# Local attention on one core: the order of the score matmuls within a slot

## Chip, core and metric

One NeuronCore of a Trainium2 chip runs the whole program. The metric is the device time of one execution in microseconds; the kernel before takes 2629.06 us (median of three runs, 2627.81 to 2631.6).

## What is computed

The input is x with 8 sequences of 256 tokens and 128 channels, 2048 tokens in all. Four blocks follow one another, each with a layer norm before and after it and a residual: additive attention, a six-layer transformer with local attention, a state-space scan, and a mixture of 8 experts. The change is in the second one. Of each of its six layers, this is the part that matters (b sequences, 16 heads of 64 dims, windows of 32 queries which see the 64 keys of their own window and the one before):

```
q, k, v = split((shift_tokens(x)) @ Wqkv)          # 128 -> 3 x 1024
q, k = rotary(l2norm(q) * qs), rotary(l2norm(k) * ksc)
sim  = einsum('bhwie,bhwje->bhwij', bq, bk2) * 8.0  # bq: (.., 32, 64), bk2: (.., 64, 64)
sim  = where(mask, -finfo.max, sim)
out  = einsum('bhwij,bhwje->bhwie', softmax(sim), bv2)
x    = out @ Wo + x
x    = ffn(shift_tokens(x)) + x                     # 128 -> 2 x 341 -> 128, gated by GELU
```

## The kernel before

Everything is in float32 unless said otherwise, with channels on partitions and tokens along the free dimension. The local-attention block works on units of 512 tokens (two sequences): 6 layers of 4 units, 24 units. A unit is worked through in 8 slots j = 0 to 7, and slot j is about the pair of heads 2j and 2j+1, of which one lies on partitions 0 to 63 and the other on partitions 64 to 127. So there are 192 slots, one score phase in each.

Each engine has its own program, written out by hand as a function `slot(i, j, ...)` (TensorE L529, ScalarE L643, GpSimd L715, VectorE L793) that is called from `iterations` (L347). The units 1 to 22 lie in a hardware loop whose body holds two units. The engines meet through semaphores alone, and each works through its list strictly as written (`need` and `gather` are waits). Work is pipelined over the slots: in slot j TensorE does the scores of pair j, the q and k projections and their norms for pair j+2, the value projection, the product with the values for pair j-2, and the transposes of pair j-1. The output projection (`wo_part`, L491) and the feed-forward part of the previous unit are spread over the slots.

TensorE in a slot, in order: `scores` (L439: two mask matmuls at L450, then the 32 score matmuls at L457); the projections `project` (L430, L431) into banks 0 and 1; `values` (L418); `mix` (L478); parts of the output projection or feed-forward (L491 to L525); `turn` (L466, transposes); `norms` (L436, L437). In slot 2 a part of L491 comes before the projections; in slot 6 L511 and `mix` do.

The score phase itself. Before it stand two waits, for the q and k of this pair (written by VectorE, L757) and for the probabilities of the pair before (written by VectorE, L781), because the score banks are used again. The two mask matmuls write the bfloat16 mask into bank 4 (head 0) and bank 5 (head 1). Each head then has 16 windows. The matmul of window w of head h takes 64 dims (partitions 64h to 64h+63) by 32 queries as weights, 64 keys as moving data, and adds into partitions 32(w mod 4) to 32(w mod 4)+31 of bank 4+h. The array is thus used in tiles of 64 rows by 32 columns: h chooses the row half, w mod 4 one of four column groups. In the trace each of these float32 matmuls is two weight loads and two matmul records, 64 of each in a slot. `mix` (L478) has two heads too, alternating; its tiles are 64 rows by 64 columns, head h in row half h and column half h, so there are two of them, and its loop is written with the head inside.

After the score phase of pair j: VectorE takes the row maximum (L765) and subtracts it (L769), ScalarE takes the exponential (L663), VectorE sums, inverts and multiplies (L776, L779, L781). ScalarE's copy of the projections (L607) and its square (L610) stand ahead of the exponential in ScalarE's list. VectorE also has the normalising product (L757) and the shuffle for the rotary embedding (L747, L750) in every slot, and in some slots residual, shift and layer-norm work. Two of these matter here: at the end of its slot 2 the residual (L816) and the shifted input of the feed-forward part (L726, L728), and at the end of its slot 5 the shifted input xs of the next unit (L726, L728), which that unit's first projection waits for (L430, in slot 6). VectorE gets to both when TensorE is already in the slot after. GpSimd does the other half of the rotary products (L709, L713).

Of the kernel before, what the change touches and what calls it, by code (L numbers as in the profile page):

```python
# [29 lines left out]
DEPTH, HEADS, DH, WIN = 6, 16, 64, 32  # L30
INNER = HEADS * DH
NP = HEADS // 2
UNIT = 512
# [11 lines left out]
def view(buf, col, *pattern, p0=0, rows=128):  # L45

    a = buf[p0:p0 + rows, 0:1]
    return bass.AP(a.tensor, a.offset + col, [[a.ap[0][0], rows]] + [list(x) for x in pattern])
# [246 lines left out]
def local_attention(nc, io, x, con):  # L295
# [9 lines left out]
    with Pool(nc) as m:  # L305
# [93 lines left out]
        def _(pe):  # L399
            def gather(sm_, value):  # L400

                if not isinstance(value, int) or value > 0:
                    pe.wait_ge(sm_, value)
                    pe.sem_inc(sem["seen"], 1)
# [34 lines left out]
            def scores(i, j):  # L439

                gather(sem["qk"], i * 8 + j + 1)
                gather(sem["p"], i * 8 + j)
                if isinstance(i, int) and i + j == 0:
                    pe.wait_ge(n1.out, n1.n + NCH)
                    pe.sem_inc(sem["seen"], 1)
                    pe.wait_ge(sem["zero"], 2)
                    pe.sem_inc(sem["seen"], 1)
                t = qk[j % 2]
                for h in range(2):
                    pe.matmul(view(ps, (4 + h) * CH, [1, 256]), identb[:, :], maskb[:, :], start=True, stop=False,  # L450
                              skip_group_check=True)
                for h in range(2):
                    for w in range(UNIT // WIN):

                        keys = (view(t, KOFF + WIN * w, [-WIN, 2], [1, WIN], p0=64 * h, rows=64) if w % 2 == 0
                                else view(t, KOFF + WIN * (w - 1), [1, 2 * WIN], p0=64 * h, rows=64))
                        mm = pe.matmul(view(ps, (4 + h) * CH + (w // 4) * 64, [1, 64], p0=WIN * (w % 4), rows=WIN),  # L457
                                       t[64 * h:64 * h + 64, WIN * w:WIN * w + WIN], keys, start=False, stop=True,
                                       skip_group_check=True)
                mm.then_inc(sem["s_mm"], 1)  # L460
# [68 lines left out]
            def slot(i, j, run, more, before):  # L529
# [4 lines left out]
                if run:  # L534
                    scores(i, j)
# [1119 lines left out]
```

## Time and profile before

| | us |
|---|---|
| median of three runs | 2629.06 (2627.81 to 2631.6) |
| span of the profiled execution | 2628.3 |
| median of the runs less this span (what lies around it) | 0.8 |
| TensorE matmul busy | 2396.4 (91%) |
| TensorE weight load busy | 1259.7 (48%) |
| VectorE busy | 1953.7 (74%) |
| ScalarE busy | 1795.4 (68%) |
| GpSimd busy | 1082.1 (41%) |

The local attention with its feed-forward runs from about 100 to 2076 us. A busy time is the union of the records of an engine. TensorE's records overlap: the next matmul of the same shape starts well before the record of the last one ends, so starts say more about its rate than lengths do.

### The profile page before, as it was taken

The numbers are of one execution on the slowest core, as the hardware profiler recorded it, in microseconds if no ns is written. First come the engines' busy times: TensorE is split into PE (matmuls) and PEld (weight loads), VectorE is DVE, ScalarE is ACT, GpSimd is POOL, SyncE is SP. The second block draws the span as 40 slices with busy tenths as digits, with TensorE's granted clock in tenths as the row PEclk, the third lists the DMA queues.
The fourth block names the chain that finished last, engine by engine and source line by source line (L and its number), as shares of the span: only waits on it lengthen the run. The fifth ranks groups of instructions, "written<-read, shape, count | busy, mean of one in ns | idle before, by whom it ended". The sixth has DMA issues, their size and how long they took to land. (4 is left out here: it accounts for less than half of the span.)

```text
span 2628.3 us, 62460 instructions
## 1 busy us (share of the span) xinstructions
PE 2396.4 (91%) x24940; PEld 1259.7 (48%) x24940; DVE 1953.7 (74%) x2595; ACT 1795.4 (68%) x2593; POOL 1082.1 (41%) x461
## 2 busy tenths in 40 slices
PE   7799999999999999999999999999999877767778
PEld 2355555555554555555545455555555422222355
DVE  5678777788677777787778777788777658999542
ACT  4677767777677776777767777677677666545533
POOL 0354444444444444444444444444444204556130
PEclk8899999999999999999999999999999989999989
DMA  0100000000000000000000000000000010000001
GB/s 21 54 2 2 2 26 10 10 2 2 15 22 11 2 2 14 22 11 2 2 14 14 19 2 2 14 14 15 5 2 2 2 37 0 0 0 0 18 23 41
DMA packets 16047, 29.92 MB, mean 11 GB/s; under 512 B 3616, under 2 KB 6064, under 8 KB 15664
## 3 DMA queue, kind: packets, MB, share of 16 engines
q1 hardware_dynamic: 15760, 25.78, 3.1%
q8 instruction: 218, 3.57, 0.5%
q14 instruction: 69, 0.57, 0.1%
HBM read 24.73 MB, written 1.05 MB: 10 GB/s over the span
## 5 line engine op out<-in xcount | busy, mean ns | idle before, releaser
L709 POOL TENSOR_TENSOR f_rot<-f_raw,f_tabc 128x1024 f32<-128x1024 f32 x192 | 452.6, 2357 | 694.7 <-DVE f_qk L757 302.4
L713 POOL TENSOR_TENSOR f_rot<-f_rot,f_shuf 128x1024 f32<-128x1024 f32 x192 | 453.1, 2360 | 470.0 <-DVE f_shuf L750 470.0
L607 ACT ACTIVATE f_raw<-f_ps 128x1024 f32<-128x1024 f32 x192 | 196.5, 1023 | 324.9 <-PE f_ps L431 324.9
L478 PEld LDWEIGHTS f_ps<-f_ptz,f_v 64*64 64x64 f32 x6144 | 260.2, 133 | 93.7 <-issue 93.7
L478 PE MATMUL f_ps<-f_ptz,f_v 64*64 64x96 f32 (+1 forms) x6144 | 286.7, 243 | 1.5 <-ACT f_ptz L628 1.4
L776 DVE TENSOR_REDUCE f_sum<-f_ps 128x8 f32<-128x512 f32 x192 | 131.8, 686 | 185.6 <-ACT f_ps L663 185.5
L747 DVE STREAM_SHUFFLE f_shuf<-f_raw 128x1024 f32<-128x1024 f32 x192 | 255.2, 1329 | 0.0
L757 DVE SCALAR_TENSOR_TENSOR f_qk<-f_rn,f_rot 128x1024 f32<-128x1024 f32 x192 | 233.5, 1216 | 28.8 <-POOL f_rot L713 28.8
L430 PE MATMUL f_ps<-f_xs,f_wq 128*128 128x512 f32 x384 | 220.7, 657 | 24.3 <-DVE f_xs L728 21.0
L750 DVE TENSOR_TENSOR f_shuf<-f_shuf,f_tabs 128x1024 f32<-128x1024 f32 x192 | 236.7, 1233 | 7.6
L616 ACT ACTIVATE f_rn<-f_ps 128x1024 f32<-128x1024 f32 x192 | 198.8, 1035 | 39.5 <-PE f_ps L437 39.0
L618 ACT ACTIVATE f_rn<-f_rn,k_lift 128x1024 f32<-128x1024 f32 x192 | 220.6, 1149 | 6.3
L457 PE MATMUL f_ps<-f_qk 64*32 64x64 f32 x12288 | 195.1, 220 | 18.0 <-issue 18.0
L1136 POOL TENSOR_TENSOR s_prod<-s_state,s_cs 128x1024 f32<-128x1024 f32 x64 | 151.7, 2371 | 145.2 <-DVE s_state L1214 145.2
L418 PE MATMUL f_ps<-f_wv,f_xs 128*64 128x256 f32 x1536 | 210.5, 395 | 0.0
L765 DVE TENSOR_REDUCE f_max<-f_ps 128x8 f32<-128x512 f32 x192 | 131.8, 686 | 105.1 <-PE f_ps L457 103.7
L610 ACT ACTIVATE f_sq<-f_raw 128x1024 f32<-128x1024 f32 x192 | 203.1, 1058 | 6.1
L436 PE MATMUL f_ps<-f_sq,f_same 128*128 128x512 f32 x384 | 197.7, 597 | 6.2 <-ACT f_sq L610 6.2
L431 PE MATMUL f_ps<-f_xs,f_wk 128*128 128x512 f32 x384 | 203.1, 611 | 0.0
L437 PE MATMUL f_ps<-f_sq,f_same 128*128 128x512 f32 x384 | 197.0, 595 | 0.0
L457 PEld LDWEIGHTS f_ps<-f_qk 64*32 64x32 f32 x12288 | 161.9, 106 | 60.2 <-issue 60.2
L491 PE MATMUL f_ps<-f_o,f_wo 128*128 128x512 f32 x384 | 183.8, 612 | 0.0
(267 smaller groups left out, 3961.4 us busy)
## 6 DMA issues: line engine op xcount, KB each, us to landing
e_w<-in_e_w SPq DMA_DIRECT2D x16, 256.0 KB, 2.8
f_wq<-in_f_wq SPq DMA_DIRECT2D x12, 256.0 KB, 2.8
f_wk<-in_f_wk SPq DMA_DIRECT2D x12, 256.0 KB, 3.2
f_wv<-in_f_wv SPq DMA_DIRECT2D x12, 256.0 KB, 3.4
f_wo<-in_f_wo SPq DMA_DIRECT2D x6, 512.0 KB, 3.1
f_w<-in_f_w SPq DMA_DIRECT2D x6, 341.0 KB, 3.1
s_dx<-in_k_pick SPq DMA_DIRECT2D x1, 1536.0 KB, 9.3
f_w<-in_f_w SPq DMA_DIRECT2D x6, 192.0 KB, 3.8
```

The lines of the kernel that those rows point to most:

```text
L418: mm = pe.matmul(view(ps, 2 * CH + 256 * r, [1, 256], p0=64 * h, rows=64), xs[:, at:at + 64], view(wv, CH * (q // 4) + 64 * h, [128, 4], [ ...
L430: pe.matmul(bank(0), wq[:, 128 * j:128 * j + 128], xs[:, :], start=True, stop=True)
L431: pe.matmul(bank(1), wk[:, 128 * j:128 * j + 128], xs[:, :], start=True, stop=True).then_inc(sem["a_mm"], 1)
L457: mm = pe.matmul(view(ps, (4 + h) * CH + (w // 4) * 64, [1, 64], p0=WIN * (w % 4), rows=WIN), t[64 * h:64 * h + 64, WIN * w:WIN * w + WIN] ...
L478: mm = pe.matmul(view(ps, 7 * CH + 64 * p, [1, n], p0=64 * h, rows=64), v[64 * h:64 * h + 64, p * CH + 64 * j:p * CH + 64 * j + 64], ptz[6 ...
L610: act.activation(sq[:, :], raw[:, :], ACT.Square).then_inc(sem["sq"], 1)
L618: act.activation(rn[:, :], rn[:, :], ACT.Exp, scale=-0.5, bias=con.lift).then_inc(sem["rn"], 1)
L709: pool.tensor_tensor(view(rot, 0, [S, 4], [1, S]), view(raw, 0, [S, 4], [1, S]), view(tab_c, 0, [S, 2], [0, 2], [1, S]), ALU.mult).then_in ...
L713: pool.tensor_tensor(rot[:, :], rot[:, :], shuf[:, :], ALU.add).then_inc(sem["rot"], 1)
L747: dve.stream_shuffle(shuf[:, :], raw[:, :], [(p + 16) % 32 for p in range(32)]).then_inc(sem["shuf"], 1)
L750: dve.tensor_tensor(view(shuf, 0, [S, 4], [1, S]), view(shuf, 0, [S, 4], [1, S]), view(tab_s, 0, [S, 2], [0, 2], [1, S]), ALU.mult).then_i ...
L757: dve.scalar_tensor_tensor(out=view(qk[j % 2], 0, [KOFF, 2], [1, UNIT]), in0=view(rn, 0, [UNIT, 2], [1, UNIT]), scalar=1e12, in1=view(rot, ...
```

## The change

Within a slot, the loop over the two heads is moved inside the loop over the 16 windows. The 32 score matmuls, their operands, their tiles and their outputs are the same; what differs is the order in which they are issued: (window 0, head 0), (window 0, head 1), (window 1, head 0), and so on, in place of 16 windows of head 0 and then 16 of head 1. The last one issued, which tells VectorE that the scores are there, is window 15 of head 1 in both.

```diff
                 for h in range(2):
                     pe.matmul(view(ps, (4 + h) * CH, [1, 256]), identb[:, :], maskb[:, :], start=True, stop=False,
                               skip_group_check=True)
-                for h in range(2):
-                    for w in range(UNIT // WIN):
+                for w in range(UNIT // WIN):
+                    for h in range(2):
 
                         keys = (view(t, KOFF + WIN * w, [-WIN, 2], [1, WIN], p0=64 * h, rows=64) if w % 2 == 0
                                 else view(t, KOFF + WIN * (w - 1), [1, 2 * WIN], p0=64 * h, rows=64))
```

## Rows read from the trace of the kernel before

**Rows 1.** Busy time by engine in the local attention (windows): length, then each engine
```profile
100.00:2076.00 1976.00, 1897.38 (x23356) 1035.79 (x23340) 1529.52 (x2128) 1465.70 (x2133) 896.91 (x381) 0.99 0.03 9
```

**Rows 2.** Groups by line, TensorE: busy us, mean ns | idle before, releaser
```profile
L478 PE MATMUL f_ps<-f_ptz,f_v 64*64 64x96 f32 (+1 forms) x6144 | 286.7, 243 | 1.5 <-ACT f_ptz L628 1.4
L457 PE MATMUL f_ps<-f_qk 64*32 64x64 f32 x12288 | 195.1, 220 | 18.0 <-issue 18.0
```

**Rows 3.** Timeline of TensorE over one slot: start, length, line, count
```profile
1045.39 0.99 PE L457 MATMUL f_ps<-f_qk 64*32 64x64 f32 x64
1046.31 1.12 PE L430 MATMUL f_ps<-f_xs,f_wq 128*128 128x512 f32 x2
...
1049.24 1.49 PE L478 MATMUL f_ps<-f_ptz,f_v 64*64 64x96 f32 x32
1050.66 0.66 PE L466 MATMUL f_ps<-f_ident,f_s 128*128 128x128 f32 x4
```

**Rows 4.** L457's matmuls in that slot, stretches from its start: length, busy (records)
```profile
1045.38:1045.66 0.28, 0.27 (x20) 1.00 0.00 0
1045.38:1045.83 0.45, 0.44 (x40) 1.00 0.00 0
1045.38:1046.17 0.79, 0.78 (x64) 1.00 0.00 0
```

**Rows 5.** L457, first 0.03 us of that phase: count, duration ns min/median/max
```profile
L457 PE MATMUL f_ps<-f_qk x4: 240/240/240, 1045.4 to 1045.4; 64*32 64x64 f32 x4
```

**Rows 6.** Records in flight in 0.01 us: of L478, then of L457 twice
```profile
1009.20:1009.21 0.01, 0.01 (x6) 1.00 0.00 0
1045.84:1045.85 0.01, 0.01 (x25) 1.00 0.00 0
1046.12:1046.13 0.01, 0.01 (x16) 1.00 0.00 0
```

**Rows 7.** Slots 1, 2, 3, 4 and 6 of one unit, as Rows 1
```profile
1349.88:1360.40 10.52, 10.46 (x125) 5.75 (x124) 6.55 (x9) 6.83 (x10) 4.96 (x3) 1.00 0.24 76
1360.40:1369.91 9.51, 9.51 (x123) 5.37 (x122) 4.34 (x8) 6.67 (x10) 4.47 (x2) 1.00 0.01 2
1369.91:1379.77 9.86, 8.91 (x122) 4.93 (x121) 9.64 (x14) 7.11 (x12) 3.90 (x2) 1.00 0.01 2
1379.77:1388.41 8.64, 8.64 (x120) 4.99 (x121) 7.71 (x12) 7.19 (x12) 5.48 (x3) 1.00 0.01 2
...
1398.00:1409.89 11.89, 10.84 (x125) 5.52 (x124) 11.43 (x19) 10.61 (x16) 5.16 (x3) 1.00 0.01 1
```

**Rows 8.** Waits over the whole span: us in total, times, longest us
```profile
DVE f_max L765 <- PE f_ps L457: 103.7, 58, 2.8
PE f_ps L450 <- DVE f_s L781: 33.6, 51, 2.4
PE f_ps L430 <- DVE f_xs L728: 21.0, 24, 5.3
PE f_ps L457 <- issue: 18.0, 10, 2.1
```

**Rows 9.** Timeline of VectorE in slots 2, 3 and 4 of that unit
```profile
1368.97 0.69 DVE L781 TENSOR_TENSOR f_s<-f_ps,f_rcp 128x512 f32<-128x512 f32 x1
...
1375.51 0.69 DVE L765 TENSOR_REDUCE f_max<-f_ps 128x8 f32<-128x512 f32 x1
...
1378.93 0.69 DVE L781 TENSOR_TENSOR f_s<-f_ps,f_rcp 128x512 f32<-128x512 f32 x1
...
1386.18 0.69 DVE L776 TENSOR_REDUCE f_sum<-f_ps 128x8 f32<-128x512 f32 x1 [0.24 <-ACT f_ps L663]
...
1387.14 0.69 DVE L781 TENSOR_TENSOR f_s<-f_ps,f_rcp 128x512 f32<-128x512 f32 x1
```

**Rows 10.** ScalarE, slot 4: the copy of the projections that the exponential stands behind
```profile
1383.02 1.02 ACT L607 ACTIVATE f_raw<-f_ps 128x1024 f32<-128x1024 f32 x1 [1.39 <-PE f_ps L431]
```

**Rows 11.** TensorE at the head of slot 0 of that unit, timeline
```profile
1338.84 0.64 PE L457 MATMUL f_ps<-f_qk 64*32 64x64 f32 x11 [1.55 <-issue]
```

## Prediction, made before the changed kernel ran

> **What bounds the kernel now.** I read the busy times first. In the local attention TensorE has a matmul under way 1897 of 1976 us, 96%, VectorE 77%, ScalarE 74%, GpSimd 45% [rows 1]. That is an average; what a shorter score phase is worth depends on whether TensorE or another engine ends last in each of the eight slots. For this the windows of one unit: in slots 1, 2 and 4 TensorE's busy time fills the slot, in slots 3 and 6 it lacks 0.95 and 1.05 us, and there VectorE is at 9.64 of 9.86 and 11.43 of 11.89 us [rows 7]. The waits name the places: the mask matmul waits 51 times for the probabilities (L781), about two per unit (slots 4 and 7), the first projection waits 24 times, once per unit (slot 6), for the shifted input (L728) [rows 8]. From the other side, VectorE's maximum waits for the score matmuls in only 58 of 192 slots [rows 8]: in the others VectorE comes late anyway. So TensorE bounds most of a unit, and VectorE two stretches of it.
>
> **What the score phase costs now.** From its first record to the start of the next group is 46.31 - 45.39 = 0.92 us [rows 3], of which 0.79 us lie before the start of the last of its 64 records [rows 4]. The starts come at three rates: 20 in the first 0.28 us (14 ns each), 20 more in the next 0.17 us (8.5 ns each), 24 in the last 0.34 us (14 ns each) [rows 4]. What does 14 ns mean? L478 has two tiles, and its 32 records, of 96 columns, take 50.66 - 49.24 = 1.42 us [rows 3], so a tile takes a record every 89 ns; by columns, a score record of 64 would want 59 ns. One head has four tiles, which gives 59/4 = 15 ns, about the 14 seen. So the first and the last stretch are one head at the speed of its four tiles, and the middle one is both heads at once. The records in flight say the same: 25 in the middle, 16 at the end [rows 6]. Head 0's 32 records at 14 ns fill 0.45 us; head 1 needs as long, but begins 0.28 us late, since it stands behind 32 others in the order.
>
> **The change part by part.** Nothing is added: 32 score matmuls in 64 records with as many weight loads, in each of 192 slots, no wait, no semaphore, no DMA. What moves is the order, and with it the idle half of the array at both ends of the phase. No other queue is passed, and the last matmul is the same, so the signal to VectorE means what it meant.
>
> The gain per slot, from both sides. If all eight tiles are fed from the first record, the phase lasts as long as one head alone, 32 x 14 ns = 0.45 us, plus a few tens of ns: the last start moves from 0.79 to about 0.48, 0.31 us saved. If instructions can't be supplied faster than in the stretch in which both heads ran, it is 64 x 8.5 ns = 0.54 us, 0.25 us saved. Since that is a rate that this order has been seen to run at, and 0.45 is one that it has not, I take 0.54, so **0.25 us per slot**. At the other end stands the loss: the nearest other phase with alternating heads, L478, has just 6 records in flight [rows 6], two tiles' worth. If alternation meant two tiles at a time here as well, 32 pairs x 59 ns = 1.89 us, 1.10 us more than now. I don't take it, because L478 has no more than two tiles to fill, while the scores have four per head, and 25 in flight in the middle stretch show more than four tiles at work. The ends are thus +1.10 and -0.31, and the value is near the second because its row is of this very phase.
>
> How many slots pass it on? I follow one unit, by what each stretch waits for.
> - Slots 7, 0, 1, 2: behind slot 7's mask TensorE has no further wait of the kinds in [rows 8] up to slot 4's mask, but for the ten breaks below; each score phase lies between two pieces of its own work. Four savings pass.
> - Slot 3: its scores don't matter. VectorE finishes the probabilities of slot 2 (L781 at 1368.97 + 0.69), then goes through shuffle, products, residual and shift and takes the maximum of slot 3 only at 1375.51 [rows 9], 4.3 us after the scores; its probabilities come at 1378.93 + 0.69, and the mask of slot 4 starts at 1379.77 [rows 7, 9]. VectorE's stretch between them has no score phase in it. It starts earlier by what was saved before, so nothing is lost either.
> - Slot 4: TensorE is full again, one saving. The other path, to slot 4's probabilities, must also come earlier: the exponential stands behind ScalarE's copy, which waits 1.39 us for the projection and so moves by the whole saving [rows 10], and VectorE's sum waits 0.24 us for the exponential [rows 9]. So that path gives 0.24, and it has room: the probabilities are there at 1387.14 + 0.69 [rows 9], 0.58 us before the mask of slot 5 at 1388.41, where slot 4 ends [rows 7].
> - Slots 5 and 6: TensorE is full in slot 5, but then waits in slot 6 for the shifted input, and that wait grows by slot 5's saving. Slot 6's scores lie before that wait too. So neither of the two passes. What was saved in slots 7 to 4 does pass through this stretch, since VectorE's list from the probabilities of slot 4 to that shift starts earlier by it.
>
> Five of eight, in 24 units: 120 savings. In ten slots the score phase breaks off after 53 records and waits for its own instructions, 18.0 us in all [rows 8], as in slot 0 of that unit, where the last 11 come 1.55 us late [rows 11]; the supply comes when it comes, and a faster start only waits longer. 110 x 0.25 = **27 us**. Against the span of 2628.3 us that is 2601; the median of the runs is 0.8 us above the span, so **2602 us**. With 0.31 us in all 120 it would be 37 us less, 2592.
>
> What could be late next is what TensorE meets sooner after a shorter phase: the projections need banks 0 and 1 free of ScalarE's reads, and the products need the spread probabilities. For the second, all of L478's idle time is 1.5 us in 192 slots [rows 2]; I take both as covered.
>
> A rule stands against all this. The first four records of the phase start within 0.03 us and all last 240 ns, where the mean is 220 [rows 2, 5]. The Trainium skill says in "TensorE: Matmul & The Clock Gate", section Part 3 (packing small matmuls), that matmuls start and end strictly in program order and that only weight loads are pulled ahead. By that rule a window's second record would wait for its first in the same tile, all behind it too, and the phase would need 32 x 59 ns = 1.9 us in either order; the change would be worth nothing. The 0.79 us measured [rows 4] speak against it: tiles evidently don't hold each other up.
>
> **The rivals.**
> - *A, no change in the phase.* If the middle stretch is fast only because a backlog of head 0 is worked off, while new instructions arrive every 14 ns, then any order takes 64 x 14 ns = 0.9 us less a backlog at the start, which is what it takes now. For it: the last 24 starts at 14 ns. Against it: they are explained by head 1's four tiles, 16 in flight [rows 6]. Time 2629.
> - *B, the phase is shorter, but less passes on.* The margins near the chain are close to the saving: 0.24 us at slot 4's sum [rows 9]. If the savings of slots 4 and 7 are lost to VectorE, three per unit less the ten stalls, 62 x 0.25 = 15.5 us, are left: 2613.
> - *C, slower: two tiles at a time.* If TensorE looks ahead less far than the eight tiles' instructions, so that a second window of the same head is not reached while the first runs, each slot loses 1.10 us. It decides from the point at which fewer than four tiles are busy. Price: 110 or more times 1.10 = 121 us, 2750. For it: L478's alternating order with 6 in flight [rows 6]. Against it: head 1's records start now while head 0 still has 12 of its 32 to go, that is over a distance of at least 12 matmuls and their weight loads.
> - *D, all eight tiles from the start.* The 37 us above, 2592. For it: four tiles do start within 0.03 us [rows 5].
>
> **How the numbers follow.** The forecast has 0.56, D 0.12, B 0.14, A 0.11, C 0.07. Measurement tells about 0.2% (5 us) from no change. Faster takes the forecast, B and D: 0.82; same 0.11; slower 0.07. The range leaves out A and C and takes in the bounds of the first three: 2589 to 2619.
>
> **What would show it.** In the changed trace L457's 64 records should start within 0.50 to 0.56 us, with 25 to 32 in flight nearly throughout; 0.79 again means A, over 1.5 us C. The busy time of L457 should fall from 195 us [rows 2] by 192 x 0.25 = 48 to about 147. The maximum's wait for the scores falls in slots 0 to 2. TensorE's waits for L781 should not fall, since slots 4 and 7 stay VectorE's, and its wait for L728, 21.0 us now, should grow by about 24 x 0.5 us, the unused savings of slots 5 and 6. If the phase is 0.25 us shorter and the time falls by less than 20 us, B holds and the sum over slots is wrong. If the time falls by more than 40 us, slots that I put on VectorE's account were TensorE's after all.

## The result and the profile after

The changed kernel takes 2613.1 us (median of 4 runs, 2611.19 to 2614.84), the kernel before in the same comparison 2629.98 us (4 runs): ratio 0.9938, 95% interval 0.9926 to 0.9949, so 13 to 19 us less. Forecast were 2602 us, with 2589 to 2619 as the range. Five more runs of the same kernel gave 2610.47 us, ratio 0.9924 (0.9911 to 0.9937) against 17 runs of before. The gain is there; it is some 17 to 19 us and not 27. One run of a later kernel (unroll_alt_1356, below) took 3398 us at a granted clock of 0.649; it is left out of every comparison, and all others agree within 0.4% with the median of their kernel.

From the page of the changed kernel, its busy times and the groups of `mix` and of the scores (busy us, mean ns | idle before):

```profile
PE 2374.6 (91%) x24940; PEld 1232.9 (47%) x24940; DVE 1954.8 (75%) x2595; ACT 1797.4 (69%) x2593; POOL 1083.0 (41%) x461
...
L478 PE MATMUL f_ps<-f_ptz,f_v 64*64 64x96 f32 (+1 forms) x6144 | 286.4, 243 | 1.5 <-ACT f_ptz L628 1.4
...
L457 PE MATMUL f_ps<-f_qk 64*32 64x64 f32 x12288 | 167.8, 225 | 19.5 <-issue 19.5
```

L457 is busy 195.1 - 167.8 = 27.3 us less than in [rows 2], 0.14 us per slot, where 48 us were forecast. The timeline of the slot that answers to [rows 3]:

```profile
1040.02 0.86 PE L457 MATMUL f_ps<-f_qk 64*32 64x64 f32 x64
1040.80 1.13 PE L430 MATMUL f_ps<-f_xs,f_wq 128*128 128x512 f32 x2
```

The next group starts 0.78 us after the first record, 0.92 before. How the 64 starts spread, as in [rows 4] (stretch from the phase's start, length, busy, records):

```profile
1040.01:1040.26 0.25, 0.24 (x32) 1.00 0.00 0
1040.01:1040.29 0.28, 0.28 (x33) 1.00 0.00 0
1040.01:1040.40 0.39, 0.39 (x38) 1.00 0.00 0
1040.01:1040.57 0.56, 0.55 (x57) 1.00 0.00 0
1040.01:1040.66 0.65, 0.65 (x64) 1.00 0.00 0
```

Half of the records start in 0.24 us, which is all eight tiles at full speed. Then there is a pause: one record up to 0.28 us, five more up to 0.39 us, and the remaining 26 in the last 0.26 us, 10 ns each. The median over the 192 phases, from first to last start, is 0.642 us after and 0.778 before: **0.136 us saved per slot**, forecast 0.25.

The slots of the unit that answers to [rows 7] (slots 1, 2, 3, 4 and 6, windows from mask to mask):

```profile
1341.60:1352.12 10.52, 10.32 (x126) 5.61 (x125) 6.60 (x9) 6.83 (x10) 4.32 (x3) 1.00 0.23 76
1352.12:1361.49 9.37, 9.37 (x123) 5.23 (x122) 4.35 (x8) 6.68 (x10) 4.53 (x2) 1.00 0.01 2
1361.49:1371.32 9.83, 8.77 (x121) 4.78 (x120) 9.61 (x14) 7.11 (x12) 3.89 (x2) 1.00 0.01 3
1371.32:1379.84 8.52, 8.52 (x121) 4.86 (x122) 7.72 (x12) 7.21 (x12) 5.37 (x3) 1.00 0.01 2
1389.42:1401.31 11.89, 10.70 (x126) 5.39 (x125) 11.43 (x19) 10.62 (x16) 5.16 (x3) 1.00 0.00 1
```

Slots 2 and 4 are 0.14 and 0.12 us shorter than in [rows 7], slots 3 and 6 are what they were, as forecast. Slot 1 is 10.52 us in both, and that was not forecast. Its TensorE busy time fell by 0.14 us and its length by nothing. The timeline of slot 1 names the reason (TensorE and ScalarE lines):

```profile
1341.60 0.38 PE L450 MATMUL f_ps<-f_maskb,f_identb 128*128 128x256 bf16 x2
...
1341.80 1.02 ACT L616 ACTIVATE f_rn<-f_ps 128x1024 f32<-128x1024 f32 x1 [0.63 <-PE f_ps L437]
...
1341.91 0.86 PE L457 MATMUL f_ps<-f_qk 64*32 64x64 f32 x64
...
1342.97 1.10 PE L430 MATMUL f_ps<-f_xs,f_wq 128*128 128x512 f32 x2 [0.20 <-ACT f_rn L616]
```

ScalarE's Ln (L616) reads banks 0 and 1, which the norms of the slot before have just filled and which the projection L430 is to write. It begins when the norms end, takes 1.02 us, and only then may L430 start. The score phase lies beside it, and a shorter one only uncovers the wait. It was the same before: in slot 1 of the unit of [rows 7] L430 also followed the Ln, 1.06 us after the first score record, where in [rows 3] it was 0.92.

```profile
1350.08 1.02 ACT L616 ACTIVATE f_rn<-f_ps 128x1024 f32<-128x1024 f32 x1 [0.63 <-PE f_ps L437]
1350.19 0.99 PE L457 MATMUL f_ps<-f_qk 64*32 64x64 f32 x64
...
1351.25 1.10 PE L430 MATMUL f_ps<-f_xs,f_wq 128*128 128x512 f32 x2
```

In the changed kernel it is 1342.97 - 1341.91 = 1.06 us again, with a score phase that is 0.14 us shorter. Over the units this stretch has the same median, 1.06 us, in slots 1 and 3 of both kernels, and goes from 0.92 to 0.79 us in slots 4 and 5. The wait now stands among the waits of the changed kernel, 47 times, in slots 1 and 3 of the units:

```profile
PE f_ps L450 <- DVE f_s L781: 34.0, 51, 2.4
...
PE f_ps L430 <- DVE f_xs L728: 24.2, 24, 5.3
PE f_ps L457 <- issue: 19.5, 10, 2.6
...
PE f_ps L430 <- ACT f_rn L616: 9.4, 47, 0.2
```

All masks of the two traces, grouped by slot, give the whole account (sum over 24 units, 23 for slot 7, since no mask follows the last one; median of units 1 to 22; worked out from the starts of L450):

| slot | before, median us | after, median us | sum saved, us |
|---|---|---|---|
| 0 | 10.48 | 10.33 | 5.6 |
| 1 | 10.52 | 10.52 | 0.0 |
| 2 | 9.51 | 9.37 | 3.1 |
| 3 | 9.84 | 9.85 | -0.3 |
| 4 | 8.65 | 8.51 | 3.2 |
| 5 | 9.58 | 9.59 | 0.0 |
| 6 | 11.89 | 11.88 | -0.1 |
| 7 | 11.24 | 11.10 | 4.4 |

Slots 2 and 4 give 24 x 0.136 = 3.3 us less a bit. Slot 7 has some 1.2 us more than its 23 x 0.136 = 3.1 us. In slot 0 the 14 units without a break give 1.8 us, about 14 x 0.136 = 1.9, and the ten others 3.8 us. So about 12 us are placed (3 x 24 + 14 = 86 savings), and the rest sits in slots 7 and 0, where the hardware loop branches back.

### The profile page after: what moved, and what is told of

The parts are those of the page before. It is cut to its first block and busy times, and to the rows that moved or that the text cites. A ratio compares the mean times of both kernels' runs of the same rounds, so it can differ in the third digit from the quotient of the medians.

```text
span 2613.1 us, 62460 instructions
## 1 busy us (share of the span) xinstructions
PE 2374.6 (91%) x24940; PEld 1232.9 (47%) x24940; DVE 1954.8 (75%) x2595; ACT 1797.4 (69%) x2593; POOL 1083.0 (41%) x461
## 5 line engine op out<-in xcount | busy, mean ns | idle before, releaser
L478 PEld LDWEIGHTS f_ps<-f_ptz,f_v 64*64 64x64 f32 x6144 | 260.1, 133 | 93.9 <-issue 93.9
L478 PE MATMUL f_ps<-f_ptz,f_v 64*64 64x96 f32 (+1 forms) x6144 | 286.4, 243 | 1.5 <-ACT f_ptz L628 1.4
L430 PE MATMUL f_ps<-f_xs,f_wq 128*128 128x512 f32 x384 | 216.1, 645 | 34.3 <-DVE f_xs L728 24.2
L616 ACT ACTIVATE f_rn<-f_ps 128x1024 f32<-128x1024 f32 x192 | 199.0, 1036 | 38.9 <-PE f_ps L437 38.6
L765 DVE TENSOR_REDUCE f_max<-f_ps 128x8 f32<-128x512 f32 x192 | 132.0, 687 | 97.7 <-PE f_ps L457 96.2
L437 PE MATMUL f_ps<-f_sq,f_same 128*128 128x512 f32 x384 | 197.0, 595 | 0.0
L457 PE MATMUL f_ps<-f_qk 64*32 64x64 f32 x12288 | 167.8, 225 | 19.5 <-issue 19.5
L418 PEld LDWEIGHTS f_ps<-f_wv,f_xs 128*64 128x64 f32 x1536 | 94.6, 138 | 164.5 <-issue 135.4
```

Source lines behind the costliest of these rows:

```text
L418: mm = pe.matmul(view(ps, 2 * CH + 256 * r, [1, 256], p0=64 * h, rows=64), xs[:, at:at + 64], view(wv, CH * (q // 4) + 64 * h, [128, 4], [ ...
L430: pe.matmul(bank(0), wq[:, 128 * j:128 * j + 128], xs[:, :], start=True, stop=True)
L478: mm = pe.matmul(view(ps, 7 * CH + 64 * p, [1, n], p0=64 * h, rows=64), v[64 * h:64 * h + 64, p * CH + 64 * j:p * CH + 64 * j + 64], ptz[6 ...
L616: act.activation(view(rn, 0, [UNIT, 2], [1, UNIT]), bank(0, 2), ACT.Ln, scale=float(2.0 ** 20)).then_inc(sem["ln"], 1)
```

## The experiments

Three questions: what sets the 0.64 us of the phase; which slots pass a saving on; and what the rest beyond 12 us is. The diffs show little more than the lines that change.

**The change once more**, unedited:

> The changed kernel once more, to set the noise. Theory S (supply): the score phase is limited by how fast its instructions come; a second trace must then show the same 0.64 us from the first to the last start of its 64 records in all slots that don't break off, since nothing else enters. The savings of 0.136 us should again lie in slots 2, 4 and 7 and in those slots 0 without a break, and none in slots 1, 3, 5 and 6; the broken slots 0 should differ from the first trace by up to 3 us either way. Rival N (the missing gain is noise): slot 1 or the phase length varies between traces. Time 2613, ratio 0.9926 to 0.9949.

2610.47 us (five runs, 2606.31 to 2610.57), ratio 0.9924 (0.9911 to 0.9937). The phase is 0.642 us again, slots 1, 2, 4 and 7 have the same medians to 0.002 us, and the sum of slot 0 differs by 3.7 us from the first trace (276.4 against 280.1). Theory N falls: neither the phase nor slot 1 varies. What varies from run to run is slot 0, and slot 6 of the very first unit (11.78 against 13.38 us).

**Half the windows**, to see the phase without its second 64 instructions. Windows 8 to 15 of both heads aren't computed in these two kernels (of the second only the new line is shown, in the place of the same two):

```diff
-                for h in range(2):
-                    for w in range(UNIT // WIN):
+                for w, h in [(w, h) for w in range(8) for h in range(2)]:
+                    if True:
```

> Windows 8 to 15 of both heads are left out (16 score matmuls, 32 records); the other windows alternate between the heads. Theory S: the first 64 instructions (32 loads, 32 records) stand ready when the phase begins and go at the tiles' speed, so the last start is 0.24 us after the first. Rival U (one rate for the whole phase, that of the changed kernel): half of 0.64 us, 0.32 us. The time of the whole is not compared; this is for the length of the phase.

```diff
+                for w, h in [(w, h) for h in range(2) for w in range(8)]:
```

> The same 16 score matmuls (windows 8 to 15 left out), first all of head 0, then all of head 1. In the kernel before, head 1 begins 0.27 us late, at its 65th instruction; here its first instruction is the 33rd. Theory S1: what is in the queue can start whatever stands before it; head 1 then starts within 0.05 us of head 0, and the order makes no difference, 0.24 us. Theory S2: TensorE reaches about 32 instructions past the oldest one that has not started; head 1 then comes in with the second round of head 0, at about 0.08 to 0.13 us, and the last start is at 0.32 to 0.36 us.

First to last start: 0.238 us alternating, 0.265 us head by head. The starts of each, alternating first (stretch from the phase's start, records):

```profile
1006.99:1007.23 0.24, 0.23 (x30) 1.00 0.00 0
1006.99:1007.24 0.25, 0.24 (x32) 1.00 0.00 0
```
```profile
1009.13:1009.40 0.27, 0.26 (x31) 1.00 0.00 0
1009.13:1009.41 0.28, 0.27 (x32) 1.00 0.00 0
```

One rate for the whole phase (0.32 us) is out. The second kernel bears on my main question. In the kernel before, head 1 comes in 0.27 us late; here, with head 0 only half as long, it comes in after 0.05 us, its 16 records then running beside head 0's. So a second head as such isn't held back. Two readings are left of why it came late in the kernel before: it stood at instruction 65 (32 loads and 32 records before it), or head 0 had too many records waiting for its four tiles. The kernel by_group, below, decides for the second. In these two half kernels, of 64 instructions each, the order is worth 0.03 us. The Trainium skill gives TensorE in "TensorE: Matmul & The Clock Gate" (the table at the head of the page) a queue of 64 instructions. The changed kernel is in line with it: its first 64 instructions, 32 records, go at the tiles' speed, the last of them starting at 0.238 us, and the next two records start at 0.27 and 0.32 us (medians of the 192 phases). That these 64 are the queue isn't shown.

**Where in the phase the order counts.** All 32 matmuls, alternating in the first or in the second half only:

```diff
+                for w, h in [(w, h) for w in range(8) for h in range(2)] + [(w, h) for h in range(2) for w in range(8, 16)]:
```

> All 32 score matmuls: windows 0 to 7 alternating, then windows 8 to 15 of head 0, then of head 1. Theory S: the first half goes as in the changed kernel (32 records by 0.24 us), then matmuls come at 17 ns each; head 0's eight take 8 x 28 ns on its four tiles, head 1's come meanwhile: last start 0.64 to 0.72 us. Theory T (tiles alone decide, supply doesn't): second half 2 x 0.22 less the overlap, 0.24 + 0.30 to 0.45 = 0.54 to 0.69 us.

```diff
+                for w, h in [(w, h) for h in range(2) for w in range(8)] + [(w, h) for w in range(8, 16) for h in range(2)]:
```

> All 32 score matmuls: windows 0 to 7 of head 0, then of head 1, then windows 8 to 15 alternating. Theory S: what comes after the first 64 instructions is bound by their arrival, 17 ns a matmul, as in the changed kernel, so the order of the first half hardly matters: last start 0.64 us, time as the changed kernel's, 2613. Theory T: the first half takes 0.32 us or more instead of 0.24, and all after it is pushed back by the same: 0.70 us or more.

Both phases last 0.686 us; one run each gave 2626.3 and 2618.5 us (2613 expected for the second), with 2630.9 us for the kernel before beside them. The two stretches of each, first_alt first:

```profile
1045.90:1046.18 0.28, 0.27 (x33) 1.00 0.00 0
1045.90:1046.60 0.70, 0.69 (x64) 1.00 0.00 0
```
```profile
1042.93:1043.21 0.28, 0.27 (x33) 1.00 0.00 0
1042.93:1043.63 0.70, 0.69 (x64) 1.00 0.00 0
```

In both, as in the changed kernel, 33 records have started by 0.28 us, although the first 64 instructions stand in different orders. After it all three go slower, and differently. For first_alt the range of theory S holds, and so, just, does that of T (0.54 to 0.69). For second_alt S said 0.64 and T at least 0.70; 0.686 is neither. That the arrival of instructions is what holds the second half fits the first half being alike, but it isn't shown, and 0.045 us of second_alt I can't explain. Of the 0.136 us, either half alone gives 0.092.

**Fewer tiles at a time**, the mechanism of my slower rival made real:

```diff
+                for w, h in [(4 * k + g, h) for g in range(4) for k in range(4) for h in range(2)]:
```

> The kernel before, but the windows ordered by column group: 0, 4, 8, 12, then 1, 5, 9, 13 and so on, heads alternating. The same 32 matmuls; eight successive ones share two tiles. Theory S with a reach of about 32 instructions (eight matmuls with their loads): two tiles work at a time, 32 pairs x 56 ns = 1.8 us from first to last start, 1.0 us more than before; in slots 0, 2, 4, 7 all of it and in the others a part passes: 2730 to 2780. With a reach of 64 instructions four tiles work, 16 rounds x 56 ns = 0.9 us: about 2645. If tiles don't matter and only the supply does, 0.64 us as in the changed kernel: 2613.

```profile
1061.99:1062.27 0.28, 0.28 (x12) 1.00 0.00 0
1061.99:1063.20 1.21, 1.21 (x64) 1.00 0.00 0
```

12 records in the first 0.28 us in place of 20, and 1.20 us in all, between the two theories' 1.8 and 0.9; the time of its one run is 2663.4 us, also between the 2730 to 2780 and the 2645 of the two. So the order can also cost, 0.42 us per slot and 33 us in all: the same matmuls, with successive ones sharing tiles. My two guesses of how far TensorE reaches past a waiting instruction (32 and 64 instructions) both miss.

The starts in this trace also tell why head 1 came late in the kernel before. A record that finds its tile unused lasts 240 ns, as the first four in [rows 5] do; one in a tile that is in use lasts 216 ns. So the records of 240 ns show when new tiles come in (medians over the 192 phases, worked out from starts and lengths; the counts are the same in at least 191 of them):

| kernel | tiles at work | records given to them | started when new tiles come in | not yet started, per tile | time, us |
|---|---|---|---|---|---|
| before | 4 | 32 | 20 | 3 | 0.27 |
| half_heads | 4 | 16 | 4 | 3 | 0.05 |
| by_group, 2nd pair of tiles | 2 | 16 | 10 | 3 | 0.26 |
| by_group, 3rd pair | 2 | 16 | 10 | 3 | 0.52 |
| by_group, 4th pair | 2 | 16 | 10 | 3 | 0.78 |

The second pair of tiles in by_group begins with instruction 33, as head 1 does in half_heads, and comes in 0.21 us later. So the place in the order doesn't decide, and the 64 instructions aren't needed to explain it. What all five have in common is the backlog: new tiles come in when the tiles ahead of them have three records each left to start. With alternating heads the first 32 records are four per tile, one running and three left, and no new tile is kept out. The pause after them in the changed kernel is another matter. Its 33rd record is the fifth of its tile, and starts at 0.27 us; in the kernel before and in by_group the fifth record of a tile starts at 0.25 us, on time. So that pause isn't the tile's, and what is left is the place behind the first 64 instructions.

**Which slots pass it on.** The value projection, which uses bank 2, goes before the q and k projections in slots 1 and 3, as it does in slot 7 already:

```diff
-                    if j == 7:
+                    if j in (1, 3, 7):
                         values(u, a)
                     project(u, a)
-                    if j != 7:
+                    if j not in (1, 3, 7):
                         values(u, a)
```

> The changed order of the scores, and in slots 1 and 3 TensorE does the value projection (L418) before the q and k projections, as it already does in slot 7. Theory P: in slots 1 and 3 the saving of the score phase is lost because the first projection waits for ScalarE's Ln (L616), which still reads banks 0 and 1; with the value projection in between, that wait is covered. Slot 1 should then be shorter by about 0.24 us (in slot 7 of the changed kernel mix starts at 4.024 us from the mask, in slot 1 at 4.268), slot 3 by nothing, since VectorE ends last there. 24 x 0.24 = 6 us: 2607. Rival Q: slot 1 is bound by ScalarE's work (copy, square, exponential), which the later projections push back by 1 us; then 2613 or more.

> The order of the scores before the change, with the value projection first in slots 1 and 3. Theory P: slot 1 gains only what TensorE waited there before the change, 4.268 - 4.160 = 0.11 us, so 24 x 0.11 = 2.6 us: 2627; and the difference to the same kernel with alternating heads is now 24 x 0.136 = 3 us larger than 17 us, because slot 1 passes its saving too: 20 us. Rival Q: no change against before, 2630, or slower, and the difference stays 17 us.

Slot 1's median: 10.28 us with alternating heads (10.52 without this edit), 10.41 us head by head (10.52). That is 0.24 and 0.11 us, to the digit what theory P said, and slot 3 is unchanged. TensorE in slot 1 of v13_alt has no wait left:

```profile
1344.98 0.86 PE L457 MATMUL f_ps<-f_qk 64*32 64x64 f32 x64
1345.77 1.08 PE L418 MATMUL f_ps<-f_wv,f_xs 128*64 128x256 f32 x8
1346.78 1.13 PE L430 MATMUL f_ps<-f_xs,f_wq 128*128 128x512 f32 x2
```

The times hardly show it: 2610.31 us (2607 expected), ratio 0.9924 (0.9907 to 0.9940), and 2629.3 us (2627 expected), 0.9999 (0.9990 to 1.0007). The first kernel's runs spread from 2600.83 to 2616.73 us, and slot 0 has 284.2 us in its trace, 4 to 8 more than in the two traces of the changed kernel. Between the two kernels lie 19.0 us by the medians, 20 expected; by the two traces it is 12.3 us from the first mask to the last, with nothing gained in slot 0 (283.4 and 284.2 us). The breaks had to go before anything of this size could be timed.

**Without the loop.** The units 1 to 22 written out in place of a hardware loop:

```diff
-            with eng.Fori(0, (LAST - 1) // 2) as pair:
-                for i in (pair * 2 + 1, pair * 2 + 2):
-                    for j in range(8):
-                        slot(i, j, True, True, True)
+            for i in range(1, LAST):
+                for j in range(8):
+                    slot(i, j, True, True, True)
```

The second kernel adds the change; the third alternates in slots 1, 3, 5 and 6 alone (`sorted(order) if j in (1, 3, 5, 6) else order`); the fourth is the second with the value projection first in slots 1 and 3.

> The order of the scores before the change; the hardware loop over units 1 to 22 is written out, so that no engine branches back. Theory B: the ten breaks in slot 0 come with the branch back at every second unit; each costs (1.12 - 0.43) us before the mask and (3.45 - 1.24) us up to the first projection, 2.9 us, 29 us in all: 2601. Rival F: the instructions come as slowly in a straight line, and breaks appear elsewhere: 2630 or slower.

> The same written-out units, with the alternating order. Theory P (the saving is 0.136 us a slot and passes in slots 0, 2, 4 and 7 alone): with no breaks it is 24 x 4 x 0.136 = 13 us against unroll_heads: 2588. If the 3 to 7 us that the change gave beyond the 12 us that I can place belong to the breaks, the difference is 13 us here; if they belong to something else in the attention, it is 16 to 20 us.

> Written-out units; the heads alternate in slots 1, 3, 5 and 6 only, the other four slots have the order before. Theory P: all four phases are 0.136 us shorter and none passes it on (slot 1 waits for the Ln at banks 0 and 1, slots 3, 5 and 6 for VectorE): the time of unroll_heads, 2601, within 1 us. Rival (my prediction's sum): slot 1 passes its saving, 3.3 us less. If all eight pass theirs, 13 us less.

> Written-out units, alternating order, and the value projection first in slots 1 and 3. Theory P: slot 1 is 0.24 us shorter again, 24 x 0.24 = 5.8 us less than unroll_alt: 2582, the fastest so far. Rival: as in the looped pair, where slot 1 was 0.24 us shorter but the whole no faster, the time stays that of unroll_alt.

| kernel | median us | ratio to before | interval |
|---|---|---|---|
| unroll_heads | 2582.69 | 0.9821 | 0.9809 to 0.9834 |
| unroll_alt_1356 | 2580.02 | 0.9812 | 0.9799 to 0.9824 |
| unroll_alt | 2570.40 | 0.9771 | 0.9758 to 0.9783 |
| unroll_v13_alt | 2565.18 | 0.9756 | 0.9743 to 0.9769 |

The ten breaks are gone and no others appear; 48 us are saved, not 29, since I had priced a break only up to the first projection, while the sum of slot 0 alone falls from 285.6 to 248.2 us, slot 7 by 6.9 and slot 6 by 5.0 us. Slot 7 is shorter only in the ten units ahead of a branch back, but slot 6 in all units 1 to 22, by 0.3 us (11.89 to 11.59); so about 5 of the 48 us aren't at the branch, and why slot 6 gains isn't shown. Here the change is worth 2582.69 - 2570.40 = **12.3 us**, against 13 worked out. By slot 0 to 7 it saves 3.5, 0.0, 3.1, -0.1, 3.2, -0.1, -0.4 and 3.1 us. Alternating in slots 1, 3, 5 and 6 alone shortens those phases too (L457 busy 178.4 us, against 191.8 and 165.1), and the sums of slots 0 to 5 and 7 stay within 0.4 us; the time is 2.7 us less, by itself nearer to the rival's 3.3. But slot 1's sum is 249.8 us in both; slot 6 has 1.5 us, all of it in the first unit, and about 1.1 us lie before the attention. The value projection first takes 5.2 us more off (5.8 expected), 4.8 of them in slot 1. Slots 1 and 2 of unroll_alt, as in the rows above:

```profile
1311.72:1322.24 10.52, 10.32 (x126) 5.61 (x125) 6.57 (x9) 6.82 (x10) 4.68 (x3) 1.00 0.23 76
1322.24:1331.61 9.37, 9.37 (x123) 5.23 (x122) 4.34 (x8) 6.67 (x10) 4.50 (x2) 1.00 0.01 3
```

The last kernel is the fastest of all, 65 us below the kernel before.

## Why the prediction came out as it did

The direction and the mechanism, more tiles at work per score phase, held, and the time lies in the range; the size was 17 to 19 us where 27 were forecast. By its steps:

- *What the three rates of [rows 4] mean.* Right as far as it went: one head is bound by its four tiles, and alternation fills the other four. The rule of strict program order among matmuls, which would have made the change worthless, is contradicted by the result too: the order made a difference.
- *The gain per slot, 0.25 us.* This is the term that was mis-sized: 0.136. I took 8.5 ns, the rate of the stretch with both heads, as one the whole phase could keep. The last records of the phase come near it, at 10 ns, but between the first 32 records and those there is a stretch from 0.24 to 0.39 us with only 6 starts, which no row of before shows. The forecast had 25 to 32 records in flight nearly throughout; there are 29 in the first stretch, but 18 and 22 in two later ones. What was missing were two things. One is why head 1 starts at 0.28 us in [rows 4]: I read it as a matter of order alone, and by_group shows that it is one of backlog, three records per tile. That part alternation removes. The other is that behind the first 64 instructions the phase goes slower in any order; that part it can't remove.
- *Slots 7, 0, 1, 2 pass.* Wrong for slot 1. I took the absence of a large wait at L430 for slack. The row was there: slot 1 in [rows 7] has 10.52 us with TensorE busy 10.46, while slot 2 has 9.51 of 9.51. That gap of 0.06 us is the wait for the Ln, already open before the change. A wait of 0.06 us is worth little by itself, and it says that a saving ahead of it on the engine gives nothing. The sentence in which I took the banks "as covered" is the one that failed.
- *Slot 4 passes, slots 3, 5 and 6 don't.* Right, shown by unroll_alt_1356 and the table. The reason for slot 5 was not quite it: of the wait for L728 I expected 12 us more, it grew by 3.2, from 21.0 [rows 8] to 24.2. That is slot 6's own saving, 24 x 0.136; slot 5's is lost before, since slot 5 has the same length in both. The place is L511 at its end, which needs what ScalarE writes in L669: from the start of L437 to that of L511 it is 0.86 us before and 0.99 us after, and L669 ends 0.09 us before L511 starts. TensorE shows 9.59 of 9.59 us busy all the same, so a full slot was no sign that a saving passes. Slot 4's other path gave as expected. Of the other signs, TensorE's waits for L781 stayed (33.6 us before, 34.0 after), and the maximum's wait for the scores fell from 103.7 to 96.2 us.
- *The ten breaks.* The savings of these slots were taken as lost. With 4 x 24 - 10 = 86 savings of 0.136 us the sum is 11.7 us. The unrolled pair shows 12.3 with all 96 (13.1 worked out). The looped pair shows 17 to 19 by its medians, so **5 to 8 us more come with the loop**; with the loop written out they are gone. That the breaks are shorter in the changed kernel is likely from this, but it isn't shown, and neither is how the order of the scores would do it: over ten breaks, the time from the last feed-forward matmul to the first projection is 45.7 us before and 43.9 and 43.3 us in the two traces after, but 42.6 us in v13_heads, which has the old order, and 42.8 in v13_alt. This stays open.
- *The rivals.* A's time is out; what it says, that the supply of instructions sets a rate, may be what holds the second half, at 10 ns and not at 14. C is out; its mechanism exists (by_group), with a price of 0.42 us and not 1.10 per slot. The distance held against it, "at least 12 matmuls", was counted in records; it is six matmuls. B's 2613 us is the time measured, but by another sum: 62 savings of 0.25 us there, 86 of 0.136 and the part from the loop here. B, that less passes on, is half of what happened, in slot 1 and not in slots 4 and 7. D's eight tiles from the first record on are there, for the first 32 records.

Two errors of the same sign, a saving of 0.136 for 0.25 and four slots for five, would have given 12 us, that is 2617 us, at the edge of the range. The 5 to 8 us that come with the loop were in no term of the sum; that the time came out 6 to 9 us inside the range is luck.

## What to carry over

When small matmuls use tiles of the array, let successive ones go to different tiles; the same 32 matmuls took 0.64, 0.78 or 1.20 us by order alone. Here other tiles came in only when those ahead had three records each left to start, so with more than four records in a row for a tile the rest of the array stays idle for a while; and what lay beyond the first 64 instructions came slower whatever the order. To see whether a saving on a full engine passes on, look for the smallest waits behind it, too, and for a group that starts later than in other slots: the engine at 10.46 of 10.52 us was bound by another one, and so was the one at 9.59 of 9.59. Moving work that needs none of the contended banks into that wait gave 5 us. Before timing changes of half a per cent, look whether a loop's branch back adds noise of the same size; writing the loop out was worth more than twice the change.

## What the runs showed that I had not expected

- In a hardware loop whose body is two units (about 2000 TensorE matmul records and as many loads), every branch back cost TensorE twice: before the mask of slot 0, and again after exactly 53 of the 64 score records, in each of the ten passes, whatever the order of the heads, by 1.3 to 2.8 us. Written out, there was none, and the kernel was 48 us faster, some 44 of them in the slots on both sides of the branches.
- A new tile is let in when the tiles ahead of it have three records each left to start: after 20 of 32 records in the kernel before, 4 of 16 in half_heads, 10 of 16 in by_group.
- Tile starts 6 to 7 ns apart: 32 records of eight tiles within 0.238 us.
- A float32 matmul record of 64 columns holds its tile for 56 ns; four column tiles of one row half run at the same time without loss, and so do two row halves that write the same partitions in different banks (29 records in flight in the changed kernel):

```profile
1040.23:1040.24 0.01, 0.01 (x29) 1.00 0.00 0
```
